# Experts' head weights split on GpSimd, result stores issued ahead of the next rows, row transfers each behind a cleared strip, the last statistics block folded into the feed-forward

## The reference

```python
x = x + ssm(ctx, layernorm(x))          # selective state space, 16 states, gated by silu(layernorm(x))
x = x + moe(layernorm(x))               # 64 experts of 512 -> 2*192 -> 512, 8 per token
x = x + cross_attention(layernorm(x), ctx)  # 16 heads of 128; q and k are RMS-normed
x = x + bitlinear_ffn(layernorm(x))       # 512 -> 2048 -> 512, ternary weights, int8 activations, gelu

def moe(x):                             # _L0_ffn_ref
    top_val, top_idx = lax.top_k(softmax(x @ gate_weight.T), 8)
    flat_e = rerouted(top_idx).reshape(-1)         # some experts are replaced by a similar one
    order = jnp.argsort(flat_e); tok = order // 8
    gu = lax.ragged_dot(x[tok], swap(gate_up_proj), group_sizes)
    gate, up = jnp.split(gu, 2, axis=-1)
    y = lax.ragged_dot(silu(gate) * up, swap(down_proj), group_sizes)
    return zeros.at[tok].add(y * w[:, None])
```

## The kernel before

| stage (function) | from | to |
|---|---|---|
| state_space | 0 | 560 |
| statistics, router_logits | 560 | 604 |
| route: ranks and positions, V values of the context; first 26 row sends | 604 | 724 |
| dispatch: K values of the context; the other 102 row sends | 724 | 902 |
| experts | 902 | 1629 |
| attention | 1629 | 2637 |
| norm_statistics (tag n3) of the last 4 tiles | 2637 | 2642 |
| feed_forward | 2642 | 2796 |

## Time and profile before

### The profile page before, as it was taken

How to read it: one execution, slowest core, us unless ns; L and a number is a source line. 1 busy time by engine, 2 the same in 40 slices (tenths; PEclk the granted TensorE clock), 3 DMA queues, 4 the chain that set the end, 5 groups by cost and what they waited for, 6 DMA issues and landing times. The chain is left out here.

```text
span 2795.7 us, 42597 instructions
## 1 busy us (share of the span) xinstructions
PE 2443.5 (87%) x11664; PEld 1826.7 (65%) x11682; DVE 1919.0 (69%) x3101; ACT 1361.7 (49%) x2693; POOL 1603.2 (57%) x1162
## 2 busy tenths in 40 slices
PE   6898987669793899999989927999999999999799
PEld 2333432267572888888889926778778777877544
DVE  6999999867463447755555556766776776566497
ACT  4566665343562444433333314555555555555377
POOL 2656565532555788877677556655664665444122
PEclk8999999989896899999999968999999999999999
DMA  6889898745676998998887464544444543343101
GB/s 200 289 268 304 271 301 278 227 149 197 237 270 229 321 327 293 318 315 309 284 298 263 153 188 133 188 132 128 158 138 138 159 157 109 104 131 106 61 24 38
DMA packets 273571, 572.68 MB, mean 205 GB/s; under 512 B 26752, under 2 KB 92416, under 8 KB 272656
## 3 DMA queue, kind: packets, MB, share of 16 engines
q1 hardware_dynamic: 188912, 373.67, 41.1%
q10 hardware_dynamic: 64032, 130.18, 13.2%
q0 software_dynamic: 20480, 67.13, 7.0%
HBM read 362.22 MB, written 208.67 MB: 204 GB/s over the span
## 5 line engine op out<-in xcount | busy, mean ns | idle before, releaser
L626 POOL TENSOR_TENSOR b_u<-du,bc 128x1024 f32<-128x1024 f32 x128 | 301.2, 2353 | 209.4 <-DVE c_state L700 113.2
L452 PE MATMUL ps_y<-c_state,ident 128*128 128x512 f32 x512 | 255.3, 625 | 87.2 <-DVE c_state L700 87.1
L2041 ACT ACTIVATE prob<-ps_s,neg,q_rs 128x512 f32<-128x512 f32 x256 | 197.1, 774 | 266.5 <-DVE neg L2231 262.9
L691 DVE TENSOR_TENSOR_SCAN state<-ps_decay,b_u 128x1024 f32<-128x1024 f32 x128 | 292.7, 2287 | 14.6 <-POOL b_u L626 2.3
L2135 POOL TENSOR_SCALAR prob<-prob,rden 128x512 f32<-128x512 f32 x256 | 175.7, 696 | 200.8 <-DVE rden L2239 200.8
L452 PEld LDWEIGHTS ps_y<-c_state,ident 128*128 128x128 f32 x512 | 93.1, 194 | 232.3 <-DVE c_state L700 139.5
L1457 PE MATMUL ps_gu<-w_gu_high,rows_t_high 128*128 (+1 forms) x636 | 231.6, 364 | 6.2 <-POOLq L1402 4.0
L524 ACT ACTIVATE ps_decay<-delta,a_neg 128x511 f32<-128x511 f32 x256 | 165.6, 681 | 140.1 <-DVE state L691 139.2
L1395 POOL TENSOR_TENSOR w_gu_low<-raw_gu,w_gu_high 128x1536 fp32r<-128x1536 f32 x63 | 220.0, 3493 | 0.0
L100 POOL DMA_INDIRECT rows_dram<-xn,pos_row x128 | 129.2, 1010 | 154.4 <-DMA rows_dram<-xn,pos_row 67.4
L1457 PE MATMUL ps_gu<-w_gu_low,rows_t_high 128*128 (+1 forms) x636 | 216.5, 340 | 0.0
(11 more groups left out here) (354 smaller groups left out, 6492.8 us busy)
## 6 DMA issues: line engine op xcount, KB each, us to landing
bc<-bc_dram SPq DMA_DIRECT2D x128, 512.0 KB
raw_gu<-in_gate_up SPq DMA_DIRECT2D x64, 768.0 KB, 5.8
rows<-rows_dram ACTq DMA_DIRECT2D x162, 256.0 KB, 4.8
y_dram<-y ACTq DMA_DIRECT2D x158, 256.0 KB, 4.2
rows_dram<-zeros SPq DMA_DIRECT2D x46, 768.0 KB
w_q<-wq_dram SPq DMA_DIRECT2D x64, 512.0 KB, 3.7
w_o<-wo_dram SPq DMA_DIRECT2D x16, 2048.0 KB, 8.6
raw_dn<-in_down SPq DMA_DIRECT2D x64, 384.0 KB, 6.9
```

Of the source, the lines that this page charges most:

```text
L452: mm = pe.matmul(ps_y[e][:, :], c.ident[:, :], c_state[:, q % 2, g, :], start=False, stop=False)
L626: pool.tensor_tensor(out=b_u[:, q % 2, :, :], in0=slot(du, n).rearrange("p (a l) -> p a l", a=1).broadcast_to([P, G, SEQ]), in1=bc[:, g % ...
L691: dve.tensor_tensor_scan(state[:, q % 2, :], decay[q % 2][:, :], b_u[:, q % 2, :, :].rearrange("p g l -> p (g l)"), 0.0, ALU.mult, ALU.add ...
L2041: act.activation(prob[:, qt, :], ps_s[qt % 2][:, :], ACT.Exp, scale=q_rs[:, k % 2, qt:qt + 1], bias=neg[:, qt:qt + 1], accum_out=den[:, qt ...
```

## The change

Four edits, in one diff.

- `send`: no wait for a landing; every send comes behind a memset of a strip of 128 x 64 on POOL and a wait for that memset.
- Experts: the split of the head weights goes to POOL, one piece after each four experts (`split_heads`), from a buffer of its own; SP loads and stores the pieces. Raw down-weights have two buffers instead of four, and gate-up and down loads are issued separately. `head_weights` and `low_heads` are gone; ACT's and DVE's unrolled part ends with iteration 30, and the last ternary store is issued behind the loop.
- ACT issues a tile's result store right behind `keep_rows`, ahead of the next row load and silu.
- The block `norm_statistics` n3 is gone. The loads of w1 (four pieces of columns, each with its semaphore) and w2 stand in feed_forward's SP program; the statistics of tiles 12 to 15 are made inside feed_forward (`late_stats` on DVE with tiles 1 to 7, `late_root` on POOL).

```diff
-EARLY, FLYING, PACED = 26, 2, 104
+EARLY, FLYING, PACED = 26, 2, NT * TOPK
+SPACE = 64
...
     if n < PACED:
-        wait(pool, m.sent[n % FLYING], 16 * (n // FLYING))
+        pool.memset(m.spacer[:, :], 0.0).then_inc(m.spaced, 1)
+        pool.wait_ge(m.spaced, n + 1)
...
-        raw_dn = p.sb("raw_dn", [FI // 2, WS, 2 * DM])
+        raw_dn = p.sb("raw_dn", [FI // 2, WS // 2, 2 * DM])
...
+            def split_heads(n):
+                pool_waits(pool, c, aw_loaded, n * 16 + 16)
+                pool_waits(pool, c, aw_stored, n * 16 + 16)
+                pool.tensor_copy(out_w[:, :, 0, :], raw_w[:, :, :]).then_inc(aw_high, 1)
+                pool_waits(pool, c, aw_high, n + 1)
+                pool.tensor_tensor(out=out_w[:, :, 1, :], in0=raw_w[:, :, :], in1=out_w[:, :, 0, :],
+                                   op=ALU.subtract).then_inc(aw_low, 1)
...
             for slot in range(1, WS):
                 expert(0, slot, first=True)
+            split_heads(0)
             with pool.Fori(1, NE // WS) as e4:
                 for slot in range(WS):
                     expert(e4, slot)
+                split_heads(e4)
...
+            def four(e4, kind, following, last=False):
+                for slot in range(WS):
+                    e = e4 * WS + slot
+                    if not last:
+                        sp.wait_ge(gu_ready, e + 1)
+                        load_gu(e + WS, slot)
+                    if not (last and slot >= WS // 2):
+                        sp.wait_ge(dn_ready, e + 1)
+                        load_dn(e + WS // 2, slot)
+                store_heads(kind, e4)
+                if following:
+                    load_heads(following, e4 + 1)
...
                     high_hidden(i, par)
                     keep_rows(i + 2, par)
+                    if not (isinstance(i, int) and i == 0):
+                        store_out(i - 1, 1 - par)
                     load_rows(i + 4, par)
                     silu(i + 1, 1 - par)
-                    if not (isinstance(i, int) and i == 0):
-                        store_out(i - 1, 1 - par)
...
-            for j in range(STATIC):
+
+            for j in range(AHEAD):
                 both(j, True)
...
             store_out(np * 2 - 1, 1)
+            store_ff(2 * NC - 1)
...
-            def low_heads(n):
-                dve.wait_ge(aw_high, n + 1)
-                dve.tensor_tensor(out=out_w[:, :, 1, :], in0=raw_heads(n), in1=out_w[:, :, 0, :],
-                                  op=ALU.subtract).then_inc(aw_low, 1)
...
+            w1 = c.ternary_dram[0].rearrange("p (k n) -> p k n", k=KD)
+            for n in range(4):
+                cols = slice(n * SEQ, (n + 1) * SEQ)
+                sp.dma_start(m.w1q[:, :, cols], w1[:, :, cols]).then_inc(w1_here[n], 16)
+            sp.dma_start(m.w2q[:, :, :].rearrange("p k n -> p (k n)"), c.ternary_dram[1]).then_inc(w2_here, 16)
...
+            def late_root(t, par):
+                if t == 5:
+                    pool_waits(pool, c, l_eps, 1)
+                    pool.tensor_tensor(out=c.rstd[:, LATE:NT], in0=l_vare[:, :], in1=c.power[:, 0:ST], op=ALU.pow)\
+                        .then_inc(l_rooted, 1)
...
+            def late_stats(t, par):
+                k = t - 1
+                if 0 <= k < ST:
+                    dve.bn_stats(l_bn6[:, k, :], c.X[:, LATE + k, :]).then_inc(l_stats, 1)
+                    dve.wait_ge(l_stats, k + 1)
+                    dve.bn_aggr(l_bn2[:, k, :], l_bn6[:, k, :]).then_inc(l_aggregated, 1)
...
-            norm_statistics(nc, c, "n3", loads, first=(BATCH - 1) * ST)
```

More of the change, by code:

```diff
@@ L1324, in experts @@
         raw_loaded = [p.sem(f"raw_gu_loaded{i}") for i in range(WS)]
-        dn_loaded = [p.sem(f"dn_loaded{i}") for i in range(WS)]
+        dn_loaded = [p.sem(f"dn_loaded{i}") for i in range(WS // 2)]
         gu_high, gu_ready = p.sem("gu_high"), p.sem("gu_ready")
@@ L1397, in expert @@
                 pool_waits(pool, c, dn_high, e + 1)
-                pool.tensor_tensor(out=flat(w_dn[1]), in0=raw_dn[:, slot, :], in1=flat(w_dn[0]),
+                pool.tensor_tensor(out=flat(w_dn[1]), in0=raw_dn[:, slot % 2, :], in1=flat(w_dn[0]),
                                    op=ALU.subtract).then_inc(dn_ready, 1)
@@ L1419, in _ @@
             sp.sem_inc(y_stored[0], 16)
             sp.sem_inc(y_stored[1], 16)
+            sp.sem_inc(aw_stored, 16)
             for slot in range(WS):
-                load_weights(slot, slot)
+                load_gu(slot, slot)
+                if slot < WS // 2:
+                    load_dn(slot, slot)
+            load_heads("w_q", 0)
             np = pairs(sp)
[L1424 to L1429, removed]
+            with sp.Fori(0, HALF - 1) as e4:
+                four(e4, "w_q", "w_q")
@@ L1430, in _ @@
+            four(HALF - 1, "w_q", "w_o")
+            with sp.Fori(HALF, 2 * HALF - 1) as e4:
+                four(e4, "w_o", "w_o")
+            four(2 * HALF - 1, "w_o", None, last=True)
+            sp.wait_ge(aw_stored, 32 * HALF + 16)
             for par in range(2):
@@ L1577, in ternary @@
                         load_ff(2 * NC + q - 1 + RS)
[L1579 to L1613, removed]
             load_rows(0, 0)
@@ L1737, in both @@
                     low_hidden(i + 1, 1 - par)
-                    if also and j < AHEAD:
+                    if also:
                         ternary(j, par)
-                    if also and j >= AHEAD and par == 1 and (j - AHEAD) % 2 == 0:
-                        low_heads((j - AHEAD) // 2)
-            for j in range(STATIC):
+            for j in range(AHEAD):
                 both(j, True)
-            with dve.Fori(STATIC, np) as j:
+            with dve.Fori(AHEAD, np) as j:
                 both(j, False)
@@ L2589, in base_hidden @@
                 return min(t + 2, NT) * 7 + t * 4
+            def late_stats(t, par):
[4 more added lines that the diff above has]
+                    dve.bn_aggr(l_bn2[:, k, :], l_bn6[:, k, :]).then_inc(l_aggregated, 1)
+                if k == ST:
+                    dve.wait_ge(l_aggregated, ST)
+                    dve.tensor_scalar(out=l_vare[:, :], in0=l_bn2[:, :, 1], scalar1=EPS, scalar2=None, op0=ALU.add)\
+                        .then_inc(l_eps, 1)
+                if k == ST + 2:
+                    dve.wait_ge(l_rooted, 1)
+                    dve.scalar_tensor_tensor(out=c.nbias[:, LATE:NT], in0=l_bn2[:, :, 0], scalar=-1.0,
+                                             in1=c.rstd[:, LATE:NT], op0=ALU.mult, op1=ALU.mult).then_inc(l_biased, 1)
             dve.tensor_copy(ident[:, :], c.ident[:, :]).then_inc(ident_made, 1)
-            schedule(dve, (1, hidden_scales), (3, add), (-1, ahead), (1, clip))
+            schedule(dve, (1, hidden_scales), (3, add), (-1, ahead), (1, clip), (1, late_stats))
 class Holder:
```

58 lines of the change are left out of this document (36 added, 22 removed).

## The result

The changed kernel takes 2838.73 us in the median of four runs (2833.20 to 2839.49), the one before 2801.56: ratio 1.0129, 95% interval 1.0105 to 1.0154. It is slower, by 37 us, where 2755 us was forecast. The profiled execution took 2839.49 us, 41.6 more than that of before.

What follows compares the result with a forecast made beforehand. PE bounds most of the kernel, but dispatch ends with its sends, leaving PE idle; sends −28, head weights and result stores −15, statistics −4 give −47 from 2797.93, 2751, raised to the runs' median: 2755 us, range 2738 to 2782.

Steps and rivals of the forecast that it cites:

- part A: Sends in route and dispatch: landing wait replaced by strip, period 1.40 us; route −7, experts start earlier, −28 us taken.
- What is late next is PE's K work and its stores: Dispatch: with sends denser, 64 K stores at 2.08 us each set the end; experts start at about 871 to 873.
- Rival 1: Dispatch: K stores slow beside back-to-back sends, K ends 13 us later; total 2768, at larger stretch 2775; chance 0.15.
- the register move of 0.348 us in place of 0.029: SP's median register move after 859.5 against before, read as a sign that back-to-back sends stretch SP's instructions.
- Rival 3: Sends: strip waits until the send's descriptors are written, period 1.90 us, total 2804 to 2812; chance 0.08.
- The 11.7 us: Dispatch's end: last send to next stage's first instruction where sends were not paced, against 4.1 us where paced.
- Part B: Experts: head-weight split moved to POOL, whose idle time hides its 55 us; −20 late, +8 early.
- −20: Experts' head-weight stretch: gain from removing ACT's casts and DVE's subtractions, between 10 us and the whole 25 us excess.
- +8: Early experts, ahead of 1212: loss from the pieces' load and store traffic, bounds 0 to 31 us.
- Part C: Experts: result store ahead of next row load and silu on ACT removes DVE's waits; −3 us (0 to −8).
- Part D: Between attention and feed-forward: statistics block removed, 4.8 us less, +1 given back; −4 us (−5 to 0).
- +1: Feed-forward: cost of four tiles' statistics on DVE, about 3.3 us that do not quite fit its 2 us free.

Runs made afterwards that it cites:

- e2: Changed kernel with the strip left out and nothing in its place, sends 1.29 us apart; 2880.9 us.
- e3: Changed kernel with the strip kept and the old wait for a landing added ahead of it, sends 1.82 us apart; 2800.9 us.
- e5: Changed kernel with the strip 128x160 instead of 128x64, sends 1.51 us apart; 2777.4 us in one run.
- e17: Changed kernel with each send moving half of each row (1 KB), sends 1.43 us apart, timed; 2763.9 us.
- e12: Changed kernel with the strip of 160 and ACT's old order in the experts (row load, silu, then result store); 2774.3 us.
- e1: Changed kernel with the old sends (landing wait up to send 104, no strip), all else changed; 2787.34 us, ratio 0.9947 to before.

## Why the prediction was wrong

**The step that failed** is in part A: "What is late next is PE's K work and its stores", costed at 2.08 us a store as before. The sends are 1.43 us apart as forecast, but beside them a K store takes 7.79 us, not 2.08. K had 17 of 64 stores out when the last send started, and the 47 left, with the stage's end, took the other 94 us: dispatch is 61.5 us longer in place of 21 shorter. With route's −5.5 (−7 forecast) part A is +56 in place of −28.

**Rival 1 named the place and not the size.** It took the last six stores of before, 2.28 us apart, as the price of back-to-back sends, and ended at 2775. In that stretch PE had 3.7 us of work left: hardly a K step stood there to be held up. Nor was the register move of 0.348 us in place of 0.029 a sign of it: in the held-up stretch of the changed kernel the same moves take 0.029 us at most. And the dense stretch was only 13 us old when K's last store left, about what the hold-up took in e2 to set in. Rival 3, the slower one, had its mechanism wrong: the strip waits for nothing. The price of a rate for *other* engines cannot be read where they have no work; a bound from above for it was never taken. The bounds that I gave to A were those of the period alone.

**The 11.7 us** behind the last unpaced send aren't a matter of pacing, as the prediction read them: they are 11.7 us in e3 and e5 too (911.2 to 922.9, 878.8 to 890.5), where every send is paced. The wait for all landings is through 2.8 us behind the last send's start, and then POOL has a DRAIN at the end of its program, 8.38 us in every trace but three with a dense tail (8.46). Before, nothing runs beside it; in the changed kernel K's work does, and the experts start 2.7 us behind the last K store. First before, then changed:

```profile
L1134 POOLq DRAIN  x1: 8379/8379/8379, 893.1 to 893.1; - x1
```
```profile
L1136 POOLq DRAIN  x1: 8379/8379/8379, 870.5 to 870.5; - x1
```

What the DRAIN waits for isn't shown. The rest of part A's sum holds once K is free: in e17, half rows at the forecast period, route is 5.9 us and dispatch 21.1 us shorter than before, −27 where −28 was forecast.

**The clock.** PE's was at 0.64 in the held-up stretch, a mix of both levels, 1.2 and 2.4 GHz; the second window's 0.95 shows it back. PE is idle in most of the stretch and its single delays are of microseconds, so I take the clock for a consequence here; no run separates it.

**Part B** was right in the head-weight stretch and too cheap ahead of it. Of −20 there, 22 were found (64 tiles × (4.55 − 4.21)); tiles 65 to 128 take 269.1 to 270.5 us in all nineteen traces of the new experts, 291.5 before. Of these 22 up to 6 may be PE's clock, 1.00 there in place of 0.98. The +8 early by traffic is 6 in this trace (295.0 − 289.0), but the first 64 tiles take 295 to 307 us in the nineteen, 300 in the median, so +11 is nearer. POOL took 16 pieces at 1.04 + 2.39 us and kept 70.6 us of idle time; PE waits no longer for POOL's weights than before. The gain fits the lock that the Trainium skill ("SBUF — State Buffer", Who interferes with whom) describes, which went with the DVE subtraction; no run tests it apart from the clock and ACT's casts. The Trainium skill's advice against two-input work on GpSimd ("GPSIMD Engine Reference", Engine selection) agrees with 2.39 against 1.21 us for 128x1024, and following the other way cost nothing here because POOL had the time. The experts' whole is −15.0 as summed, where other traces of the same experts give 713 to 724 us, so −4 to −15.

**Part C**: 3 us forecast, none found (e12). The waits that it removed were, as far as these runs tell, off the path.

**Part D**: the block's 4.8 us went, as forecast. The statistics among the tiles cost more than the +1: from the first operation on a tile to the end it is 2837.8 − 2680.80 = 157.0 us, before 2795.7 − 2642.45 = 153.3, so 3.7 us are given back and D is about −1 in place of −4. In the other traces these 157.0 us are 155.8 to 157.2. That is about the whole of what the operations take (3.3 us by my count), as if DVE had no room to hide them.

B, C and D together are −15.6 us by medians (e1) where −19 were forecast.

## What to carry to other kernels

Before making one engine's transfers denser, ask what the other engines do beside them, and price it where they have work and for long enough: a short stretch at the end of a stage, where the dense rate already runs, shows nothing if the others are done. If a pacing wait is to go, keep its distance and test the rate in steps; here 0.08 us more between sends (the strip 160 instead of 64) turns 37 us lost into 31 gained. Don't settle on the limit's edge: at 1.455 us K was held up in one build on one chip and free in another on two others, at 1.50 us never, on four chips.

## What was not expected of the hardware

Indirect row transfers issued by GpSimd every 1.43 us (128 rows of 2 KB, 0.97 us of GpSimd each) slow the K work of all the other engines beside them by a factor of almost four (stores 7.8 us apart in place of 2.1), and every 1.29 us by five; at 1.51 us they do nothing. At 1.29 us it took about ten transfers until it set in. The transfers' own data move as ever (the last packet of a send ends 2.4 us behind its start in the changed kernel and 3.0 in e5, medians) and the DMA is only 0.55 busy, so DMA bandwidth isn't it. What resource is full stays open. A late semaphore alone would not hold back the transposes that wait for none, and the missing semaphore events of the records are no guide. Every run here was recorded, so that the recording itself takes part isn't excluded. Whether the limit lies lower when a send has fewer bytes, or differs from chip to chip, or both, isn't settled; half again as many bytes in the stores of another queue didn't bring the hold-up on at its full size.

Behind its last indirect transfers of this stage GpSimd spends 8.38 us in a DRAIN, whatever the period, which costs the stage that long when nothing else is left to do.
